# Sixteen instead of eighteen adj trees ahead of the attention tiles, with six trees in tiles 0 to 3

## What is computed

```python
q = x @ Wq.T + bq
k = key @ Wk.T + bk
v = value @ Wv.T + bv
scores = einsum('nd,md->nm', q, k) / N ** 0.5
adj_scores = scores * adj
adj_scores = where(abs(adj_scores) < 1e-05, -1e9, adj_scores)
prob = softmax(adj_scores, axis=-1)
out = layernorm(x + (prob @ v) @ Wm.T + bm)
```

## Time and profile before

| | us |
|---|---|
| median of 3 runs | 539.13 |
| lowest and highest | 537.80, 539.78 |
| the profiled execution, its own time | 536.55 |
| its span from the first to the last instruction | 534.8 |

### The profile page before, as it was taken

How to read it: one execution, slowest core, us unless ns; L and a number is a source line. 1 busy time by engine, 2 the same in 40 slices (tenths; PEclk the granted TensorE clock), 3 DMA queues, 4 the chain that set the end, 5 groups by cost and what they waited for, 6 DMA issues and landing times.

```text
span 534.8 us, 5719 instructions
## 1 busy us (share of the span) xinstructions
PE 507.8 (95%) x1684; PEld 267.4 (50%) x1684; DVE 302.5 (57%) x759; ACT 229.8 (43%) x463; POOL 240.0 (45%) x242
## 2 busy tenths in 40 slices
PE   6999999999999599999999999999999999999693
PEld 3444444444444255555555555555565555556362
DVE  0056452985039046677877888765556444535354
ACT  0233312333333143444744653664564374466284
POOL 4010004007750053777656765566556554656400
PEclk9999999999999799999999999999999999999898
DMA  8999999999999997999999998367456445456413
GB/s 324 335 218 260 282 270 240 210 268 317 294 378 289 296 342 300 240 294 306 276 301 318 242 290 293 109 202 255 126 187 215 154 151 170 108 186 199 114 40 121
DMA packets 44196, 127.25 MB, mean 238 GB/s; under 512 B 9981, under 2 KB 10237, under 8 KB 38018
## 3 DMA queue, kind: packets, MB, share of 16 engines
q0 software_dynamic: 21696, 71.82, 53.0%
q1 hardware_dynamic: 16082, 34.97, 17.7%
q10 hardware_dynamic: 6384, 20.06, 9.7%
HBM read 161.98 MB, written 25.17 MB: 350 GB/s over the span
## 4 chain that ended last, share of the span: by engine, by line
PE 75%; DVE 10%; ACT 6%; DMA 5%; issue 4%; DVEq 0%; ACTq 0%
PE bank L507 21%; PE bank L516 15%; PE bank L623 12%; PE bank L644 11%; PE bank L597 5%; DMA big<-xT 4%; PE bank L543 3%; PE bank L557 3%; PE bank L633 2%; PE bank L614 1%; PE bank L566 1%; DVE big L942 1%; DVE score L1080 1%; ACT size L829 1%; ACT keyT L817 1%
## 5 line engine op out<-in xcount | busy, mean ns | idle before, releaser
L516 PE MATMUL bank<-big,M 128*128 128x512 f32 x256 | 122.3, 606 | 4.6 <-DMA big<-xT 4.6
L390 POOL DMA_INDIRECT kv<-table,index x84 | 88.3, 1051 | 81.8 <-PE bank L644 58.0
L425 POOL DMA_INDIRECT adj_g<-adj_cols,index x96 | 98.4, 1025 | 29.3 <-issue 29.0
L507 PE MATMUL bank<-y_buf,big 128*128 128x512 f32 x256 | 111.3, 594 | 0.0
L623 PE MATMUL bank<-keyT,qT 128*128 128x384 f32 x256 | 88.7, 490 | 3.1 <-issue 1.9
L644 PE MATMUL bank<-kv,probT 128*128 128x512 f32 x186 | 86.8, 603 | 4.3 <-issue 4.3
L507 PEld LDWEIGHTS bank<-y_buf,big 128*128 128x128 f32 x256 | 48.2, 190 | 60.6 <-issue 59.6
L623 PEld LDWEIGHTS bank<-keyT,qT 128*128 128x128 f32 x256 | 47.9, 190 | 41.0 <-issue 13.3
L942 DVE TENSOR_TENSOR big<-big 128x2048 bf16<-128x2048 bf16 x32 | 38.9, 1216 | 51.0 <-DMA big<-adj_tiles 51.0
L516 PEld LDWEIGHTS bank<-big,M 128*128 128x128 f32 x256 | 45.4, 195 | 41.9 <-issue 41.9
L402 POOL DMA_DIRECT2D big<-adj_tiles x32 | 18.2, 570 | 106.8 <-PE bank L507 63.0
(11 more groups left out here) (106 smaller groups left out, 533.4 us busy)
## 6 DMA issues: line engine op xcount, KB each, us to landing
big<-adj_tiles POOLq DMA_DIRECT2D x32, 1024.0 KB
big<-valueT ACTq DMA_DIRECT2D x8, 1024.0 KB
x_buf<-x SPq DMA_DIRECT2D x32, 256.0 KB
table<-key SPq DMA_DIRECT2D x8, 1024.0 KB
out<-y_buf SPq DMA_DIRECT2D x31, 256.0 KB
big<-xT SPq DMA_DIRECT2D x6, 1024.0 KB
table<-qT ACTq DMA_DIRECT2D x5, 1024.0 KB, 24.3
table<-y_buf ACTq DMA_DIRECT2D x3, 1024.0 KB
```

What stands on the lines that cost most here:

```text
L390: pool.indirect_dma_start(kv[:, b, c, :], None, table, bass.IndirectOffsetOnAxis(index[:, t, c:c + 1], 0), bounds_check=N - 1, oob_is_err= ...
L425: pool.indirect_dma_start(adj_g[:, b, c, :], None, adj_cols, bass.IndirectOffsetOnAxis(index[:, t, CH + c:CH + c + 1], 0),).then_inc(adj_g ...
L507: mm = nc.tensor.matmul(bank[4 + t % 2][:, :], col_buf[nb % 2][:, d, k * P:(k + 1) * P], G[:, d, :], start=(d == 0), stop=(d == DC - 1))
L516: mm = nc.tensor.matmul(ps[:, :], M[:, d, a * P:(a + 1) * P], col_buf[nb % 2][:, d, :], start=(d == 0), stop=(d == DC - 1))
```

## The change

`FIRST` becomes 16 and a list names the trees of each tile. `value_sums()` keeps its place behind tree 15.

```diff
-        FIRST = 18
+        FIRST = 16
+        TREES = [[16], [17, 18], [19], [20, 21]] + [[t] for t in range(22, T)]
...
         def trees_of(i):
 
-            return [FIRST + i] if FIRST + i < T else []
+            return TREES[i] if i < len(TREES) else []
...
             for t in range(FIRST):
                 reduce_tile(t)
-                if t == FIRST - 3:
+                if t == FIRST - 1:
                     value_sums()
```

## The result

The changed kernel is slower by 0.77%: the ratio of its time to the time before is 1.0077, 95% interval 1.0057 to 1.0097. The medians are 541.73 us (20 runs) and 538.5 us (20 runs). The profiled execution took 539.62 us with a span of 537.8 us, where the one before took 536.55 with 534.8. So the two traces differ by 3.0 us of span, and most of the loss can be looked for in them.

A forecast was written before the change was run, and what follows sets the result against it. TensorE, 95% busy, was taken as the bound, its front limited by the 16 DMA engines. The front gives 0.6 to 2.3 us, `gather(4)` caps it at 1.7, VectorE about 0: 539.13 - 1.5 = 537.6 us, range 534.6 to 542.0.

The forecast's parts named there:

- Later gathers have more room: Gathers behind `gather(4)`: GpSimd's groups follow each other by 8.45 us, the tiles by 10.56, so load 20 costs nothing there.
- 2.8 us earlier: End of the key copies: load 20 taken out gives 4.8 us, less 2 for idle engines; bounds 4.8 earlier, 1 later.
- xT's wait goes: Front, near 175 us: TensorE's 4.6 us wait for xT's second block and 3.3 us of low clock vanish, 7.9 us.
- The wait moves to `values(0)` and the clock with it: At `values(0)`: a new 4.9 us wait leaves 4.0 of 7.9 us; low clock takes 1.7 to 3.4, leaving 0.6 to 2.3.
- the last value store, like the copies, gains about 4 us (bounds 0 and 5): Last store of value rows into `table` lands about 4 us earlier, so its gathers land for `values(0)` at 197.8.
- The hole: Loads 16 and 17 leave 132 to 149: about 5 us idle per typical engine; the slowest's backlog fills all but 2.
- `gather(4)` behind two loads: Tile 4: with load 20 also ahead it lands at 226.3, TensorE wants it at 227.97; caps the gain at 1.7 us.
- VectorE's cover: Tiles 1 and 3: the second trees hide, in tile 3 with 0.3 us to spare; otherwise up to 2.1 us lost.
- rival 1: At `values(0)`: the last value store lands no earlier, 8.9 us idle plus low clock, 3.1 us slower, 542.2 us; chance 0.15.
- Rival 2: Slowest DMA engine's lag shrinks: copies end near 207, `gather(4)` lands at 223.5, front's 4.0 us survive, 535.1 us; chance 0.22.
- Rival 3: Front hardly changes, xT still near 178; double load shows at `keys(4)`, 0 to 1.5 us slower, 539.9 us; chance 0.12.

The follow-up runs named there:

- load 20 alone: Kernel before with adj load 20 issued behind the wait for the key copies, ahead of load 21 and `gather(4)`: ratio 0.9992.
- after, second trace: The changed kernel itself, unedited, run again in another group on one chip: ratio 1.0045 to the kernel before, 534.1 us.
- the key copies sooner: Changed kernel with the eight key copies released four value units earlier, at 24 units done instead of 28: ratio 1.0058 to the kernel before.
- xT later: Changed kernel with the load of xT's fourth block issued one tile later: ratio 1.0028 to the kernel before.
- the kernel at 0.9961: Changed kernel with loads 16 and 17 back between the early gathers, 18 and 19 behind them: ratio 0.9961 to the kernel before.
- 0.995 and 0.990: Load 20 behind the key copies, then one load ahead of each gather, two in step 6: 0.995 with trees of before, 0.990 with the changed kernel's.
- the other pair: Changed kernel with loads 16 and 17 between gathers and one load a step, without and with key copies four value units earlier: 0.9949 and 1.0015.

## Why the prediction was wrong

The forecast was 537.6 us, 1.5 us faster than before and so no change that can be measured. The kernel is 3.2 us slower (541.73 us, 0.77%). That lies inside the stated range of 534.6 to 542.0, and on the other side of before.

**The step that failed.** It is "Later gathers have more room": the sum let load 20 cost nothing behind `gather(4)`. It cost most, at tile 5. In five traces two loads stand ahead of `gather(4)` and TensorE waits for the keys of tile 5. The last column is the time from one to the other:

| kernel | load behind the key copies starts, us | `keys(5)` starts, us | between, us |
|---|---|---|---|
| trees of after, loads 16 and 17 between the gathers | 206.22 | 236.21 | 29.99 |
| load 20 alone | 207.68 | 237.64 | 29.96 |
| after, second trace | 211.29 | 241.37 | 30.08 |
| after | 211.72 | 241.72 | 30.00 |
| GpSimd's queue of after, trees of before | 212.10 | 242.12 | 30.02 |

So `keys(5)` follows the end of the key copies by 30.0 us, whatever the front and VectorE did. (Two more kernels have this queue, those with the key copies sooner and with xT later. TensorE doesn't wait for `keys(5)` in either: it comes late from `values(0)`.) Before, `keys(5)` started at 237.22 without a wait. Had the copies ended 2.8 us earlier, at 209.8, as forecast, `keys(5)` would by this have started at 239.8 (an estimate): 2.6 us slower, where the sum had 1.5 us faster. The copies ended only 0.9 us earlier, which adds 1.9 us. Together that is the ledger's +4.5 at tile 5. The second error is thus the term "2.8 us earlier" for the key copies.

Of the signs that the prediction named, xT's wait, the full clock there, the wait at `values(0)` with the low clock behind it and the wait at tile 4 came. The value gathers (189.58 for 186 to 187) and the load behind the copies (211.72 for 209 to 211) were too late.

**xT's wait goes: right.** Also its 3.3 us of low clock: `keys(0)` comes 5.1 us earlier. The forecast had 7.9. Most of the rest is the 2.43 us of waiting for ScalarE. In the second trace, without that wait, `keys(0)` stands at 179.34, 7.7 us earlier. ScalarE started a copy at 156.18 after 6.61 us without work and so issued xT's block at 160.57 instead of 157.77. Its timeline after:

```profile
156.18 0.60 ACT L759 ACTIVATE y_buf<-bank 128x512 f32<-128x512 f32 x1 [6.61 <-remote]
...
160.57 0.33 ACTq L750 DMA_DIRECT2D big<-xT  x1
161.19 0.38 ACTq L764 DMA_DIRECT2D table<-y_buf  x1
```

The profile names no cause. It isn't needed for the loss: the second trace of the changed kernel doesn't have this wait, and its ratio is 1.0045. Two other kernels with the early gathers in one row, those with the key copies sooner and with xT later, have it (1.94 and 2.11 us of TensorE); three don't. The three traces with it come from the groups of runs with the waits at tile 29, the four without it from the two other groups, and the changed kernel is in both. So the change alone doesn't make it, and what delays ScalarE stays open.

**The wait moves to `values(0)` and the clock with it: right as a mechanism, wrong in size.** The term is "the last value store, like the copies, gains about 4 us (bounds 0 and 5)". It gained 1.0, and 1.5 in the second trace. It was the furthest off and yet didn't set the time: at `keys(2)` TensorE still stood 0.4 us earlier than before (forecast 0.6 to 2.3), and `keys(5)` hung on the copies. The wait was 3.85 us against a forecast of 4.9 only because TensorE came later than forecast; in the second trace it was 6.32. The low clock behind it cost 4.51 - 2.81 = 1.7 us for the six matmuls (2.1 in the second trace, 4.87).

**The hole: why the copies gained 0.9 and not 2.8 us.** "Its backlog fills all but some 2 us of the hole" was read from the slowest engine. Measured by undoing each part, from the start of the load behind the key copies: load 20 away gives 4.9 us (212.61 to 207.68), as forecast (4.8). Loads 16 and 17 behind take 3.1 us (212.61 to 215.70); with load 20 away they take 4.4 us with the trees of before (207.68 to 212.10) and 5.1 with those of after (206.22 to 211.29). So the hole costs 3 to 5 us, and the copies end 0.9 us earlier instead of 2.8. The window 141 to 147 shows the hole itself: (1 - 0.65) x 6 = 2.1 us of idle time on a mean engine, on top of the stretches beside it. The bounds named for the copies, 4.8 earlier and 1 later, held.

**Why the store gains as little as the copies.** In 174 to 180 after, the three queues moved as many packets each:

```profile
q0 software_dynamic: 139, 1.01, 80.1%
q1 hardware_dynamic: 136, 0.26, 12.6%
q10 hardware_dynamic: 139, 0.28, 12.3%
```

The equal counts say that they take turns, packet for packet, and nearly all of GpSimd's packets are the 8 KB ones. Per engine that is 8.7 turns in 6 us, 0.69 us a turn. While loads are queued, the value store on ScalarE's queue gets one 2 KB packet in such a turn. Its end therefore goes by the number of loads that are queued beside it, as within each set of the table, and after has four there where before had three: 16 and 17 came, 20 went. That it landed 1.0 us earlier and not later may come from the earlier start of the loads (152.97, all four in a row); no run took that apart. An estimate from these rows: a load lasts 8 turns; a turn without one is (6 us x 16) / 369 = 0.26 us, so a load delays the store by 8 x (0.69 - 0.26) = 3.4 us. The table of starts gives 5.5 and 4.9 us for the second and the third load, 1.5 to 2.1 more than the estimate, which stays unexplained. The Trainium skill (DMA: Bandwidth & Descriptors, Queues, rings and completion order) says that each engine goes round the queue rows it has work for, a packet at a time; the counts agree, 139, 136 and 139.

The prediction counted work ahead of the store as one sum in which 16 and 17 were there already. They had been: but in 129 to 149, where they filled a stretch that nothing else fills, and not beside the store.

**`gather(4)` behind two loads: right as a mechanism, too short.** 1.85 + 0.40 us at tile 4, forecast 0 to 2. The prediction's own sum with the copies as measured gives 224.3 + 4.8 - 0.9 = 228.2; the adj part came at 230.05. With load 20 alone it gives 224.3 + 4.8 - 4.9 = 224.2, and it came at 225.97. So 1.8 us are missing in that sum both times, and no row says where. The sum used it as a cap on a gain; since the front had given its gain away by then, it was a loss of 1.9 us in the ledger.

**"Later gathers have more room": wrong.** `gather(5)` is issued at the same time as before, but the queue ahead of it holds one load more. Behind load 22 it was still moving when SyncE's xT block came at 228.62 (229.07 before, where it did no harm), and TensorE got its keys at 241.72 (the chain of after, from GpSimd's issue on):

```profile
221.93 1.04 POOL kv L391
223.27 0.99 POOL kv L391
224.57 17.10 DMA kv<-table,index
241.72 1.53 PE bank L598 x12
```

With the 0.40 us for the adj part this is most of the ledger's step from +1.5 to +4.5. The step compared GpSimd's rhythm of 8.45 us with the tiles' 10.56, but the rhythm of issue is not that of landing, and a transfer on another queue took 43% of the engines' time in 233 to 240. The experiment with xT later (1.0028) takes back 0.2 to 0.5% of it, if it may be set beside the changed kernel's ratios of other groups, 1.0045 and 1.0077.

**VectorE's cover: right.** No wait for VectorE in tiles 1 to 5 of either trace of after. There TensorE is late in tile 4 anyway; in the kernel at 0.9961, where it isn't, it has no such wait either. The three pairs of kernels that differ only in the trees (0.9992 and 0.9961; 1.0084 and 1.0045 or 1.0077; 0.995 and 0.990) have the doubled trees on the faster side, the first two pairs across chips.

**The rivals.** In size it ended as rival 1 (542.2). That rival turned on the last value store landing no earlier, and asked for a gain under 1 us; it was 1.0. But it had the whole loss ahead of `values(0)`, while the ledger has it at tiles 4 and 5. Rival 2, the slowest engine relieved, fell: GpSimd still waits 6.22 us for the copies. Rival 3's term at tile 4 came in addition to the forecast's chain, not in place of it; it was wrong to let each case have only one wait.

What stays open is why ScalarE starts late, in the front and at tile 29, in some groups of runs, and where the 1.8 us at `gather(4)` come from.

## What to carry to other kernels

A term that a sum uses only as a cap on the gain can turn out as a loss. Follow the moved transfer through every later wait on its queue: here GpSimd's chain from the end of the key copies to `keys(5)` was 30.0 us long in five traces of four kernels, and a faster front didn't shorten it. Count the large transfers that are queued beside a small one that somebody waits for, not the bytes ahead of it: here the 8 KB packets of one queue and the 2 KB packets of the others went in equal numbers. Put large loads into the stretches that only small, issue-bound transfers would use otherwise, here between the early gathers: that place alone was worth 3.7 and 4.1 us in two pairs. A load that is put off is paid for at the next gather on its queue, so spread such a debt over several, one a step, and look for what other queues start at that moment.

## What the hardware showed that was not expected

- A 1 MB load on GpSimd's queue moved the landing of a store on ScalarE's queue by about 5 us for the second and again for the third: 180.19, 185.7 (mean of three traces) and 190.59.
- Filling a stretch in which the engines were idle (share 0.65 to 1.06) did not shorten anything (1.0058 against 1.0077 and 1.0045): the earlier copies delayed the value gathers by 3.1 us, and by 4.5 us (185.15 to 189.63) in the other pair, where there was no hole to fill.
- The early gathers on GpSimd keep the engines busy only if something else is queued: at 1.0 us each and 0.30 us between them, the share fell to 0.65 without adj loads (141 to 147 us), at 204 GB/s.
- ScalarE can start a copy 6.6 us after its last work though TensorE needs it 2.4 us earlier, and the profile has no cause for it.
- Such late starts go with the group of runs. At tile 29 they make TensorE wait 3.5 to 5.3 us in all eight traces of the groups in which the kernel before took 536.9 to 538.5 us. None of the eight traces of the groups in which it took 531 to 532 us has them.
